# A two-layer graph network on one core: a new order of the normalisation's steps on VectorE and ScalarE

## The chip, the cores and the metric

The kernel runs on one core of one Trainium2 chip. The metric is the time of one execution in microseconds (us) on the device, lower is better. Five engines run side by side, each through its own list of instructions in order: TensorE (PE in the profile; PEld are its weight loads), VectorE (DVE), ScalarE (ACT), GpSimd (POOL) and SyncE (SP), which here issues nearly all DMAs. They are tied together by semaphores only: an instruction may wait until a semaphore has reached a count, and increments one when it ends.

## The reference

There are 1250 nodes of 512 features and 40000 edges. Cut to what matters:

```python
h = relu(layernorm(x))                                   # h0, layer 1's input
msg = (h[src] + edge_attr) @ Wm.T + bm
agg = segment_sum(msg, dst) / max(deg, 1)
o = h + gelu(concat(h, agg) @ Wu.T + bu)
x1 = x + layernorm(o) * gamma + beta
h1 = relu(layernorm(x1))                                 # layer 2's input
rst = (1 + eps) * h1 + segment_sum(h1[src], dst)
out = x1 + h1 + relu(rst @ W1 + b1) @ W2 + b2
```

All data is float32, and layernorm subtracts the mean and divides by sqrt(var + 1e-5) over the 512 features of a node.

## The kernel before

The nodes are cut into NT = 10 tiles of 128 rows (the last has 98). The kernel has four stages in time.

1. Up to about 243 us: a loop over 79 groups of 512 edges. TensorE sums the edge rows by destination and counts the edges between each pair of nodes into a 1280 x 1280 matrix of counts, A. The sums over neighbours of both layers are products with A (`piece`, `times_A`).
2. From 247 to 326 us: the normalisation, around which the change lies. Here all engines work tile by tile.
3. Up to 343 us: what is left of layer 2's products with A.
4. Up to the end: the two dense products of layer 2 (L1454, L1470), and the output.

In stage 2 TensorE's order is written out by hand (L1410 to L1437). For each tile b it runs `map_agg(b)` (L1401), the aggregate times the combined weights. From b = 5 on this is followed by `transpose_h1(b - 5)` (L1386) and, from b = 6, `times_A(b - 6, "A")` (L1377, L1378). Then, with the ten map_agg done, TensorE waits once for `t_ready` 10, that is for update(9), and for b = 5 to 9 runs `transpose_h1(b)`, `times_A(b - 1, "A")`, and one or two `times_A(.., "B")` as filler. `transpose_h1(b)` waits for h1(b); `times_A(b)` waits for low_h1(b), through the semaphore split1.

VectorE and ScalarE run software-pipelined rounds k. In each round they go through a fixed list of steps, each with a lag: a step with lag 2 works in round k on tile k - 2. For one tile the way is:

- VectorE `update` (L1017) forms t; ScalarE `gelu` (L627) and `h0_again` (L623, h0 once more from x, which SyncE loads again at L396).
- VectorE `add_h0` (L1022), `o_moments`, `o_moments2`, `o_variance` (L1026, L1030, L1034); GpSimd takes the power -1/2 (L463); VectorE `center` (L1038), and `add_x` (L1048), which gives x1 with the sum of its row; beside these, `add_beta` (L1042) makes x + beta ready.
- VectorE `x1_moments` (L1053) turns the row sum into minus the mean. ScalarE `x1_squares` (L632) sums the squares of x1 less its mean. VectorE `x1_variance` (L1057) waits for that sum; GpSimd takes the power (L460); VectorE `shift` (L1061) multiplies mean and power.
- ScalarE `h1` (L637) waits for shift and writes layer 2's input; `h1_high` (L641) rounds it to a high part. TensorE transposes it; ScalarE `h1T` (L646) copies the transpose; VectorE `low_h1` (L1066) makes the low part that times_A needs.

The lists of before, in their order, with the lags in brackets: ScalarE gelu (0), h0_again (0), x1_squares (2), h1 (3), h1_high (3), h1T (3); VectorE update (0), center (2), x1_variance (3), add_h0 (1), add_x (2), o_moments (1), x1_moments (2), shift (3), add_beta (1), o_moments2 (1), o_variance (1), low_h1 (4). So for one tile b ScalarE makes the squares in round b + 2 and h1 in round b + 3; VectorE makes x1_moments in its round b + 2, and variance and shift in its round b + 3. A step whose tile is out of range is left out: update and gelu end with round 9.

The waits of the steps that move:

```python
            def x1_variance(b):
                dve.wait_ge(x1_square, b + 1)
            def shift(b):
                dve.wait_ge(rs2_ready, b + 1)
            def x1_squares(b):
                act.wait_ge(x1_mean, b + 1)
            def h1(b):
                act.wait_ge(nb2_ready, b + 1)
                act.wait_ge(x1_square, b + 1)
```

Of the kernel before, what the change touches and what calls it, by code (L numbers as in the profile page):

```python
# [30 lines left out]
def gnn_kernel(nc, x, src, dst, edge, Wm, bm, Wu, bu, gamma, beta, W1, b1, W2, b2, eps, out):  # L31
# [20 lines left out]
    NX = NP // XW  # L52
    WU_ORDER = list(range(FC, 2 * FC)) + list(range(FC))
    assert ETAIL % 2 == 0 and ETAIL <= GE // 2 and D == GE and FC == 4 and sum(n for _, n in QS) == NP
    assert len(QS) == 3 and QS[2][1] * 2 == 512 and KW <= 256 and NT == 10

# [160 lines left out]
    with ctx:  # L217
# [198 lines left out]
        def _(pool):  # L416
# [16 lines left out]
            def add_sums_of(n):  # L433
                _, loaded = nc.values_load_multi_w_load_instructions(
                    offrow[0:1, n * 4:n * 4 + 2].bitcast(I32), engines=(mybir.EngineType.Pool,), min_val=0, max_val=(NP << 16) - 1,
                    skip_runtime_bounds_check_because="a pair of least indices of nodes")
                for half, first in enumerate((loaded[0] & 0xFFFF, loaded[0] >> 16)):
                    first = nc.s_assert_within(first, 0, NP - 1, skip_runtime_bounds_check_because="each is the least of indices of nodes")
                    cols = aggT[:, :, bass.ds(first, W)]
                    if half == 0:  # L440
                        pool.wait_ge(turned_out, n + 1)
                    if n > 0 or half > 0:
                        pool.wait_ge(early_step, n * 2 + half)
                    sums = turned_sums[n % TURNS][:].rearrange("p (f q) -> p f q", f=FC)[:, :, half * QUAD:half * QUAD + W]
                    nc.gpsimd.tensor_tensor(cols, sums, cols, ALU.add).then_inc(early_step, 1)  # L445
# [31 lines left out]
        def _(act):  # L477
# [138 lines left out]
            def full_conv(c):  # L616
                nc.scalar.copy(AR[:, c, :], A16[:, c, 0:NP]).then_inc(conv, 1)
# [35 lines left out]
            for c in range(1, CONV_AHEAD):  # L653
                full_conv(c)
            for k in range(NT + 4):
                for work, lag in ((gelu, 0), (h0_again, 0), (x1_squares, 2), (h1, 3), (h1_high, 3), (h1T, 3)):
                    if work is h0_again and k < 2:
                        continue
                    if 0 <= k - lag < NT:
                        work(k - lag)  # L660
                for c in range(CONV_AHEAD + 2 * k, min(CONV_AHEAD + 2 * k + 2, NT)):
                    full_conv(c)
# [15 lines left out]
        def _(dve):  # L678
# [68 lines left out]
            def offsets(n):  # L747
                _, loaded = nc.values_load_multi_w_load_instructions(
                    offrow[0:1, n * 4:n * 4 + 2].bitcast(I32), engines=(mybir.EngineType.DVE,), min_val=0, max_val=(NP << 16) - 1,
                    skip_runtime_bounds_check_because="a pair of least indices of nodes")  # L750
                return [nc.s_assert_within(first, 0, NP - 1, skip_runtime_bounds_check_because="each is the least of indices of nodes")
                        for first in (loaded[0] & 0xFFFF, loaded[0] >> 16)]
# [255 lines left out]
            def packed(first):  # L1008
                return ps[:, first:first + 2, :].rearrange("p k (g n) -> p (k g) n", g=2)

            def add_sums(products, start):
                part = aggT[:, :, start:start + products.shape[-1]]
                return V.tensor_tensor(part, products, part, ALU.add)
# [49 lines left out]
            def low_h1(b):  # L1063
# [4 lines left out]
            dve.wait_ge(late_in, 48)  # L1068
            dve.wait_ge(deg_step, 3 + NT)

            STEPS = [(update, 0), (center, 2), (x1_variance, 3), (add_h0, 1), (add_x, 2), (o_moments, 1), (x1_moments, 2), (shift, 3), (add_beta, 1),
                     (o_moments2, 1), (o_variance, 1), (low_h1, 4)]
            for k in range(NT + 5):
                if k == 5:
                    dve.wait_ge(piece_mm, 3 * NT)
                    add_sums(packed(0)[:, :, 0:LAST], QS[2][0]).then_inc(agg_done, 1)
                for work, lag in STEPS:
                    if 0 <= k - lag < NT:
# [28 lines left out]
        def _(pe):  # L1107
# [323 lines left out]
            for _, b in filler:  # L1431
                last = times_A(b, "B")
# [66 lines left out]
```

## Time and profile before

| | us |
|---|---|
| time, median of 3 runs | 483.59 (482.88 to 483.61) |
| the profiled execution's own time | 483.73 |
| its span in the trace | 481.9 |
| TensorE busy | 468.1 |
| VectorE busy | 260.6 |
| ScalarE busy | 172.0 |
| GpSimd busy | 123.3 |

The span runs from the first to the last instruction of the trace; some 1.8 us of the execution's time lie around it. Busy time is the sum over an engine's instructions, overlaps counted once. In a timeline each row gives the start of an instruction and its duration in us, the engine, the line of the kernel, the operation, what it writes and reads, and in square brackets how long its engine had been idle before it and what ended that. Instructions of one engine overlap a little: the next starts some 0.06 to 0.08 us before the end that is shown for the one before it. So the time that a step takes in its engine's row of work is read from start to start.

### The profile page before, as it was taken

To read this page: it belongs to the slowest core of one execution; us is meant where nothing else is said; L and a number is where in the kernel's file an instruction comes from. 1 tells how busy PE (TensorE), PEld (TensorE's weight loads), DVE (VectorE), ACT (ScalarE), POOL (GpSimd) and SP (SyncE) were. 2 spreads that over 40 slices of the span, in tenths; PEclk is the share of its full clock that TensorE was granted. 3 is DMA by queue.
4 is the path that set the end of the run, shared out by engine and by line. 5 is a ranking of instruction groups with operands and counts; after the bars stand their busy time and mean duration, and the time that the engine had idled before them with its cause. 6 is when DMAs were issued, how large, how long until landed. Compare 5 with 4: busy or idle time off the path is not lost.

```text
span 481.9 us, 9420 instructions
## 1 busy us (share of the span) xinstructions
PE 468.1 (97%) x3313; PEld 282.3 (59%) x3313; DVE 260.6 (54%) x615; ACT 172.0 (36%) x332; POOL 123.3 (26%) x185
## 2 busy tenths in 40 slices
PE   6999999999999999999999999899999999999997
PEld 5555555454555455788765755799744449444445
DVE  4799887778787877997847599822000000011011
ACT  6677642333333337521049387920021213000000
POOL 4016434443343422000000232449980000000000
PEclk9999999999999999999999999999999999999999
DMA  8999999999999999999430111030220000010111
GB/s 280 377 395 407 409 387 387 406 389 403 394 387 402 407 396 382 345 347 339 167 89 22 44 45 40 28 148 1 74 101 0 0 0 1 22 44 23 44 44 38
DMA packets 31832, 98.92 MB, mean 205 GB/s; under 512 B 3686, under 2 KB 4906, under 8 KB 31786
## 3 DMA queue, kind: packets, MB, share of 16 engines
q1 hardware_dynamic: 30570, 97.27, 53.4%
q10 hardware_dynamic: 1216, 1.05, 0.7%
q8 instruction: 27, 0.44, 0.4%
q14 instruction: 19, 0.16, 0.1%
HBM read 95.76 MB, written 2.56 MB: 204 GB/s over the span
## 4 chain that ended last, share of the span: by engine, by line
PE 89%; DVE 3%; issue 3%; DMA 2%; DVEq 1%; ACT 1%; SPq 0%; POOL 0%; ACTq 0%; POOLq 0%
PE ps L1470 14%; PE ps L1454 14%; PE ps L1185 11%; PE ps L1401 7%; PE ps L1234 7%; PE ps L1204 6%; PE ps L1377 4%; PE ps L1378 4%; PE ps L1295 4%; PE ps L1213 4%; PE ps L1296 4%; PE ps L1193 3%; PE ps L1137 3%; DMA WmN<-in_L_gnn_Wm_dram 2%; DVE A L760 1%
## 5 line engine op out<-in xcount | busy, mean ns | idle before, releaser
L445 POOL TENSOR_TENSOR aggT<-turned_sums,aggT 128x88 f32 x118 | 61.3, 520 | 96.7 <-ACT turned_sums L518 83.7
L760 DVE TENSOR_TENSOR A<-ps,A 128x220 f32 x158 | 60.8, 385 | 33.0 <-PE ps L1204 24.1
L1098 DVE TENSOR_TENSOR U<-ps,U 128x512 f32<-128x512 f32 x9 | 6.2, 692 | 122.3 <-PE ps L1470 122.3
L1470 PE MATMUL ps<-W2s,hid 128*128 128x512 f32 (+1 forms) x176 | 68.9, 553 | 0.0
L1454 PE MATMUL ps<-aggT,W1s 128*128 (+1 forms) x192 | 67.3, 513 | 0.0
L1185 PE MATMUL ps<-ea,oneD 128*22 128x256 f32 x944 | 62.6, 383 | 3.1 <-issue 2.8
L1454 PEld LDWEIGHTS ps<-aggT,W1s 128*128 128x128 f32 x192 | 36.4, 190 | 30.7 <-issue 30.6
L1470 PEld LDWEIGHTS ps<-W2s,hid 128*128 128x128 f32 (+1 forms) x176 | 32.6, 185 | 36.0 <-issue 34.5
L1185 PEld LDWEIGHTS ps<-ea,oneD 128*22 128x22 f32 x944 | 23.3, 101 | 50.0 <-issue 25.3
L512 ACT COPY packed_sums<-ps 128x256 f32<-128x256 f32 x59 | 22.0, 372 | 80.7 <-PE ps L1185 80.5
L1377 PE MATMUL ps<-AR,Hh 128*128 128x256 f32 (+2 forms) x160 | 43.8, 310 | 0.0
L1378 PE MATMUL ps<-AR,Hl 128*128 128x256 f32 (+2 forms) x160 | 43.0, 305 | 0.0
L739 DVE TENSOR_TENSOR oneK<-iotaP,P_key 128x1760 bf16<-128x1760 bf16 (+1 forms) x40 | 42.6, 1064 | 0.0
L669 ACT ACTIVATE hid<-ps,b1C 128x512 f32 (+1 forms) x24 | 14.6, 608 | 77.7 <-PE ps L1454 77.7
L1204 PE MATMUL ps<-oneK,oneS 128*128 128x220 bf16 x316 | 40.9, 260 | 0.4 <-DVE A L760 0.4
L1234 PE MATMUL ps<-Wu1T,U 128*128 128x512 f32 x80 | 41.3, 598 | 0.0
L1401 PE MATMUL ps<-CT,aggT 128*128 128x512 f32 x80 | 35.5, 592 | 0.0
L1295 PE MATMUL ps<-ARc,Hh 128*128 128x512 f32 x80 | 32.8, 410 | 0.7 <-DVE Hl L794 0.7
L1204 PEld LDWEIGHTS ps<-oneK,oneS 128*128 128x128 bf16 x316 | 29.9, 97 | 2.8 <-issue 1.0
L1296 PE MATMUL ps<-ARc,Hl 128*128 128x512 f32 x80 | 31.6, 394 | 0.0
L1378 PEld LDWEIGHTS ps<-AR,Hl 128*128 128x128 f32 x160 | 30.2, 189 | 1.7
L1377 PEld LDWEIGHTS ps<-AR,Hh 128*128 128x128 f32 x160 | 30.2, 189 | 1.6
(152 smaller groups left out, 631.5 us busy)
## 6 DMA issues: line engine op xcount, KB each, us to landing
ea<-in_edge_attr_dram SPq DMA_DIRECT2D x78, 1024.0 KB, 8.7
X<-in_x_dram SPq DMA_DIRECT2D x1, 2304.0 KB
xt<-in_x_dram SPq DMA_DIRECT2D x9, 256.0 KB, 2.5
out_dram<-U SPq DMA_DIRECT2D x9, 256.0 KB
W1s<-in_L_gnn_W_dram SPq DMA_DIRECT2D x1, 2048.0 KB, 9.0
W2s<-in_L_gnn_W_dram SPq DMA_DIRECT2D x1, 2048.0 KB, 8.4
Wu2N<-in_L_gnn_Wu_dram ACTq DMA_DIRECT2D x2, 512.0 KB, 4.2
WmN<-in_L_gnn_Wm_dram SPq DMA_DIRECT2D x1, 1024.0 KB, 7.3
```

The costliest lines, as they stand in the source:

```text
L445: nc.gpsimd.tensor_tensor(cols, sums, cols, ALU.add).then_inc(early_step, 1)
L760: V.tensor_tensor(cols, ps[:, 4 + m % 2, half * KW:(half + 1) * KW].rearrange("p (h w) -> p h w", w=W), cols, ALU.add).then_inc(add_step, 1)
L1185: last = T.matmul(to.rearrange("p (c d) -> p c d", c=2), oneD[h][:, g * 2 + j, :], data, start=j == 0, stop=j == 1)
L1204: last = T.matmul(ps[:, 4 + m % 2, (j // 2) * KW:(j // 2 + 1) * KW], sources[:, j // 2, :, j % 2], keys[:, j // 2, :, j % 2], start=j % 2 ...
L1234: quarter = T.matmul(ps[:, ASIDE_BANK["u1", b], :], U[:, b, f * P:(f + 1) * P], Wu1T[:, f, :], start=f == 0, stop=f == FC - 1)
L1295: T.matmul(to, Hh[:, c, rows], here, start=c == 0 and (q < 2 or f % 2 == 0), stop=False)
L1296: last = T.matmul(to, Hl[:, c, rows], here, start=False, stop=c == NT - 1 and (q < 2 or f % 2 == 1))
L1377: T.matmul(to, Hh[:, b, rows], AR[:, b, start:start + cols], start=b == 0 and (cols == 512 or f % 2 == 0), stop=False)
L1378: last = T.matmul(to, Hl[:, b, rows], AR[:, b, start:start + cols], start=False, stop=b == NT - 1 and (cols == 512 or f % 2 == 1))
L1401: last = T.matmul(ps[:, 2 + b % 2, :], aggT[:, f, b * P:(b + 1) * P], CT[:, f, :], start=f == 0, stop=f == FC - 1)
L1454: last = T.matmul(ps[:, CHUNK_BANK[k % 4], 0:cols], W1s[:, f, k * P:(k + 1) * P], aggT[:, f, bass.ds(start, cols)], start=f == 0, stop=f = ...
L1470: last = T.matmul(ps[0:rows, Y_BANK[b + half], 0:cols.stop - cols.start], hid[:, k, b * P:b * P + rows], W2s[:, k, cols], start=k == 0, st ...
```

## The change

Two lists are reordered, and nothing else changes: the same instructions, the same waits and the same data.

- ScalarE: x1_squares (of tile k - 2) moves behind h1 and h1_high (of tile k - 3).
- VectorE: x1_variance (k - 3) moves ahead of center; shift (k - 3) moves from behind x1_moments to ahead of add_x; x1_moments (k - 2) moves ahead of o_moments, to directly behind add_x.

```diff
-                for work, lag in ((gelu, 0), (h0_again, 0), (x1_squares, 2), (h1, 3), (h1_high, 3), (h1T, 3)):
+                for work, lag in ((gelu, 0), (h0_again, 0), (h1, 3), (h1_high, 3), (x1_squares, 2), (h1T, 3)):
...
-            STEPS = [(update, 0), (center, 2), (x1_variance, 3), (add_h0, 1), (add_x, 2), (o_moments, 1), (x1_moments, 2), (shift, 3), (add_beta, 1),
+            STEPS = [(update, 0), (x1_variance, 3), (center, 2), (add_h0, 1), (shift, 3), (add_x, 2), (x1_moments, 2), (o_moments, 1), (add_beta, 1),
                      (o_moments2, 1), (o_variance, 1), (low_h1, 4)]
```

## Rows read from the trace of the kernel before

**Rows 1.** The page's busy times: engine, busy us, share of the span, instructions.
```profile
PE 468.1 (97%) x3313; PEld 282.3 (59%) x3313; DVE 260.6 (54%) x615; ACT 172.0 (36%) x332; POOL 123.3 (26%) x185
```

**Rows 2.** Busy time of stages 2 and 3 together, with TensorE's granted clock (1.00 is full).
```profile
247.00:343.50 96.50, 94.28 (x523) 70.47 (x522) 57.96 (x139) 54.43 (x90) 38.83 (x38) 1.00 0.13 46
```

**Rows 3.** Timeline of TensorE: map_agg, transposes, first matmuls of times_A, tiles 1 to 8.
```profile
277.05 3.60 PE L1401 MATMUL ps<-CT,aggT 128*128 128x512 f32 x8
280.62 0.66 PE L1386 MATMUL ps<-ident,X 128*128 128x128 f32 x4
...
292.16 0.60 PE L1386 MATMUL ps<-ident,X 128*128 128x128 f32 x4
...
297.90 0.60 PE L1386 MATMUL ps<-ident,X 128*128 128x128 f32 x4
...
301.96 0.63 PE L1386 MATMUL ps<-ident,X 128*128 128x128 f32 x4 [1.59 <-issue]
...
306.00 0.66 PE L1386 MATMUL ps<-ident,X 128*128 128x128 f32 x4 [0.63 <-ACT X L637]
306.41 0.48 PE L1377 MATMUL ps<-AR,Hh 128*128 128x512 f32 x1
...
309.63 0.48 PE L1377 MATMUL ps<-AR,Hh 128*128 128x512 f32 x1
...
313.76 0.48 PE L1377 MATMUL ps<-AR,Hh 128*128 128x512 f32 x1
```

**Rows 4.** Timeline of ScalarE, round 7's h1T(4) and round 8.
```profile
298.54 0.69 ACT L646 ACTIVATE aggT<-ps,eps 128x512 f32<-128x512 f32 x1 [1.77 <-PE ps L1386]
...
300.35 0.71 ACT L632 ACTIVATE X<-U,mv 128x512 f32<-128x512 f32 x1
...
301.06 0.80 ACT L637 ACTIVATE X<-U,nb,rs 128x512 f32<-128x512 f32 x1
301.89 0.62 ACT L641 CAST Hh<-X 128x512 fp32r<-128x512 f32 x1
```

**Rows 5.** Timeline of VectorE, round 9: update(9) to low_h1(5).
```profile
299.23 0.74 DVE L1017 SCALAR_TENSOR_TENSOR tt<-ps,rdeg,U 128x512 f32<-128x512 f32 x1
299.89 0.74 DVE L1038 SCALAR_TENSOR_TENSOR tt<-tt,mv,gammaB 128x512 f32<-128x512 f32 x1
301.19 0.15 DVE L1057 TENSOR_SCALAR ve<-mv 128x1 f32<-128x1 f32 x1 [0.56 <-ACT X L632]
...
301.88 0.74 DVE L1048 SCALAR_TENSOR_TENSOR U<-tt,rs,xt 128x512 f32<-128x512 f32 x1
...
302.55 0.69 DVE L1026 BATCH_NORM_STATS2 stats<-tt 128x6 f32<-128x512 f32 x1
...
304.16 0.69 DVE L1066 TENSOR_TENSOR Hl<-X,Hh 128x512 fp32r<-128x512 f32 x1
```

**Rows 6.** Timeline of ScalarE, a cast with an operation right behind it.
```profile
218.03 0.62 ACT L562 CAST ARc<-A 128x512 fp32r<-128x512 uint16 x1 [1.25 <-PE ps L1296]
218.56 0.20 ACT L601 ACTIVATE eps<-epsC 128x1 f32<-128x1 f32 x1
```

**Rows 7.** Timeline of VectorE, low_h1(6) and round 11.
```profile
308.38 0.69 DVE L1066 TENSOR_TENSOR Hl<-X,Hh 128x512 fp32r<-128x512 f32 x1
308.99 0.74 DVE L1038 SCALAR_TENSOR_TENSOR tt<-tt,mv,gammaB 128x512 f32<-128x512 f32 x1
309.65 0.15 DVE L1057 TENSOR_SCALAR ve<-mv 128x1 f32<-128x1 f32 x1
309.77 0.75 DVE L1048 SCALAR_TENSOR_TENSOR U<-tt,rs,xt 128x512 f32<-128x512 f32 x1
...
310.57 0.15 DVE L1053 TENSOR_SCALAR mv<-x_sum 128x1 f32<-128x1 f32 x1
310.97 0.16 DVE L1061 TENSOR_TENSOR nb<-mv,rs 128x1 f32<-128x1 f32 x1 [0.25 <-POOL rs L460]
```

**Rows 8.** The page's DMA issues, second load of x: KB each, us to landing.
```profile
xt<-in_x_dram SPq DMA_DIRECT2D x9, 256.0 KB, 2.5
```

## The prediction, made before the changed kernel ran

> **What bounds the kernel now.** I read the page's busy times first, then the stage table, then the timelines of stage 2. TensorE is busy 97% of the span [rows 1]: only its idle time can be won, and a wait of another engine costs only what reaches TensorE. In stages 2 and 3 it is idle for 96.50 - 94.28 = 2.22 us, at the full granted clock of 1.00, its level of 2.4 GHz [rows 2]. The timeline shows where: 1.59 us before the transposes of tile 5, 0.63 us before those of tile 6, and before those of tile 1 a gap of 0.13 us that the matmuls' modelled ends hide (map_agg takes 3.44 us from start to start, 277.05 + 3.44 = 280.49, and they start at 280.62) [rows 3]. The first is marked "issue", but h1(5) ends at 301.06 + 0.80 = 301.86 and the transposes start 0.10 us later [rows 3, 4]: all three wait for ScalarE's h1. All three gone would give 2.35 us.
>
> So two chains matter. ScalarE is tied to TensorE: h1T(4) follows the transposes' start by 0.64 us, the three steps h1T, gelu and h0_again take 1.81 us, squares 0.71, h1 0.83 up to h1_high [rows 3, 4]. VectorE is nearly full too: in round 9 it idled 0.56 us, and that in x1_variance(6), which waited for squares(6): it starts 0.84 us after they do [rows 4, 5]. low_h1(6) starts at 308.38, is visible at about 308.38 + 0.69 + 0.10 = 309.17, and times_A(6) needs it at 309.63 [rows 3, 7]. Only 0.46 us of slack are there.
>
> **The change, part by part.** No instruction is added or removed. On ScalarE h1 comes 0.71 us earlier behind h0_again, the place of the squares. In return the squares come behind h1 and h1_high: 0.83 us plus the pitch from h1_high to the next operation. That pitch isn't in the trace, since h1T waits there; a cast of the same size was followed after 0.53 us [rows 6], and the upper bound is h1_high's whole 0.62 us. I take 0.53, so the squares are late by 1.36 us, less what the round as a whole gains.
>
> On VectorE x1_variance moves ahead of center, so it wants the squares 0.66 us earlier (299.23 to 299.89, one step of this size [rows 5]) and gets them later. Behind the blocked x1_variance stand center, add_h0, shift, add_x, the moments, add_beta, low_h1 and the next update. TensorE waits for two of these: update(9) and low_h1. The rest of the round: from x1_variance to low_h1 it took 304.16 - 301.19 = 2.97 us [rows 5]; center (0.66) now lies within; and x1_moments stands directly behind add_x, whose sum it needs: 310.57 - 309.77 = 0.80 us, where o_moments follows after 0.67 (301.88 to 302.55), so 0.13 more [rows 5, 7]. Together 3.76 us. shift needs GpSimd's power, 310.97 - 309.65 = 1.32 us after x1_variance [rows 7]; center, the 0.06 us of x1_variance and add_h0 (0.60, as low_h1's 0.61 [rows 7]) cover 1.32 to 1.33 of that, so I take no wait. If the power came 0.1 to 0.2 us later, each round would pay that; earlier wins nothing.
>
> On x1_moments the Trainium skill says otherwise (VectorE: DVE Perf Modes, section "The DRAIN you can't avoid"): a chain of operations with a semaphore after each took as long as one without. By that rule the move would cost 0.00 instead of 0.13 us in each of two rounds and the sum below would be 0.26 us less. The row of 0.80 us decides, since here the value comes from a second instruction that reads the accumulator.
>
> Now step by step, in the times of the trace. The transposes of tile 1 lose their wait of 0.13 us; TensorE is then unbroken up to tile 4's.
> - Tile 3's transposes at 292.16 - 0.13 = 292.03. The chain to VectorE is 0.64 + 1.81 + 0.83 + 0.53 + 0.84 = 4.65 us: x1_variance(5) at 296.68, low_h1(4) at 300.44, update(9) at 301.05, done at 301.79.
> - Tile 4's transposes at 297.77. h1(5) starts at 297.77 + 0.64 + 1.81 = 300.22 and ends at 301.02, so it no longer holds TensorE. Tile 5's transposes wait for t_ready 10 instead: 301.79 + 0.10 = 301.89, 0.07 us earlier than before. The wait has changed its owner.
> - x1_variance(6) at 297.77 + 4.65 = 302.42 (before 301.19). low_h1(5) at 306.18 (before 304.16).
> - h1(6): h1T(5) at 302.53, h1(6) at 304.34 to 305.14. TensorE comes free at 301.89 + 3.41 = 305.30 (the 3.41 from 301.96 to 306.00 less 0.63): transposes of tile 6 at 305.30, 0.70 us ahead of before. This is the change's gain.
> - times_A(5) could start 0.41 us later, at 305.71, but low_h1(5) is visible at 306.18 + 0.79 = 306.97: 1.26 us of new idle time, now 0.56 us behind before.
> - Round 10: squares(7) allow x1_variance(7) at 304.34 + 0.83 + 0.53 + 0.84 = 306.54, VectorE arrives at 306.18 + 0.61 = 306.79. low_h1(6) at 310.55, visible at 311.34. TensorE is at times_A(6) at 306.97 + 3.22 = 310.19 (3.22 from 306.41 to 309.63 [rows 3]): 1.15 us more idle time. times_A(6) at 311.34 against 309.63: 1.71 us late.
> - Round 11: x1_variance(8) at 311.16, shift(8) 1.32 us later, add_x(9) after 0.07, x1_moments(9) after 0.80, low_h1(7) at 313.40, visible at 314.19. TensorE wants it at 311.34 + 4.13 = 315.47 (309.63 to 313.76 [rows 3]). No wait there, nor at tile 8, where h1(8) starts at 312.66 behind shift(8): x1_variance(9) at 314.86, shift(9) at 316.18, low_h1(8) visible at 317.0 against 319.6.
>
> After that TensorE runs on without idle time, so 1.71 us stay. What else the late VectorE moves is covered. update(7) runs by about 290.3 (x1_variance(4), one tile of 5.74 us before 296.68, less 0.66), and map_agg(9) wants it at about 294.3. The load of x for tile 9, on SyncE behind add_x(6), is issued about 299.3 and lands 2.5 us later [rows 8], and h0_again(9) wants it at 303.6. W1's load, queued behind add_x(9), and GpSimd's additions behind low_h1(9) shift by 2 to 3 us and are wanted only after 343 us.
>
> Sum: profiled execution 483.73 + 1.71 = 485.44 us. The median of the runs is 0.14 us under that execution, so 485.3 us. Bounds of this sum: x1_moments at 0.67 instead of 0.80, -0.26; the pitch behind h1_high at 0.62, +0.09; power late by 0.2 us in two rounds, +0.4. That makes 485.0 to 485.8.
>
> A measurement of this kernel can tell about 0.2% (0.97 us) from no change: the bounds are 482.62 and 484.56 us.
>
> **The rivals.**
> 1. The change works as built: VectorE's delay never reaches TensorE, h1 is earlier and that counts. Place: low_h1(5) and (6). It decides where x1_variance stalls VectorE by under about 0.7 us in all. For it: rows 5 show only 0.56 us of stall now, and h1 is the one releaser that the profile names. Against it: the squares move by 1.36 us and the step that wants them by 0.66 the other way, and 0.46 us of slack is left. Time: the 0.70 us won at tile 6 stay, 483.59 - 0.70 = 482.9; all three gaps gone, 483.59 - 2.35 = 481.2. Chance 0.08, half of it below 482.62.
> 2. VectorE is late only once: it makes up the second stall, because the squares start sooner than my chain says, and times_A(6) finds its low part at 310.2. Then +0.56 to +0.8 stays: 484.2 to 484.4. Chance 0.08.
> 3. GpSimd's power becomes the bound of VectorE's rounds. The cover of 1.32 us equals the power's 1.32 us; with 0.3 us more in rounds 8 to 11 update(9), low_h1(5) and (6) shift in turn, +0.9 to +1.2 beyond my sum: 486.3. Chance 0.10.
> 4. The clock: two stalls of 1.26 and 1.15 us close to each other, and TensorE falls to its 1.2 GHz level. For it: no such pair is in the trace; against it: 1.59 and 0.63 us passed at 1.00. Price, an estimate: one tile of 4.13 us doubled, 485.3 + 4.1 = 489.4. The Trainium skill (TensorE: Matmul & The Clock Gate, Part 1) has such a fall after idleness. Chance 0.02.
>
> **How the numbers follow.** My forecast has 0.72, all of it slower. Rivals 3 and 4 are slower as well: 0.84. Rival 2 and half of rival 1 lie within 0.2%: 0.12. Faster: 0.04. The range takes in my bounds, the upper half of rival 2 and most of rival 3: 484.2 to 486.5.
>
> **What would show it.** x1_variance (L1057) waiting for ScalarE's squares earlier in the stage too, over 1 us for tile 2, and some 0.7 us in each of rounds 8 and 9; transposes of tile 5 released by update (L1017), those of tile 6 without an idle time of any size; times_A (L1377) with two new waits for low_h1 (L1066), each over 1 us; TensorE's idle time in stages 2 and 3 at about 3.9 us instead of 2.2. Wrong would be my forecast if L1377 shows no wait, or if L1061 waits for GpSimd in each round.

## The result, and the profile after

The changed kernel takes 485.51 us (median of 6 runs, 485.25 to 485.67) beside 483.65 us (6 runs) for the kernel before on the same chip: ratio 1.0038, 95% interval 1.0028 to 1.0049. It is slower, by 1.86 us. I had forecast 485.3 us. The profiled execution took 485.67 us, its span 483.9 us.

The page's busy times of the changed kernel, and then the row of its stage table for stages 2 and 3 (busy time of each engine in a stretch of the trace), answering to [rows 1, 2]:

```profile
PE 469.0 (97%) x3313; PEld 282.7 (58%) x3313; DVE 261.1 (54%) x615; ACT 171.9 (36%) x332; POOL 124.0 (26%) x185
```

```profile
247.00:345.60 98.60, 95.12 (x524) 71.00 (x523) 58.99 (x140) 54.28 (x90) 39.23 (x38) 1.00 0.14 45
```

Every engine has as many instructions as before. TensorE's idle time in stages 2 and 3 rose from 2.22 to 98.60 - 95.12 = 3.48 us, and the granted clock stayed at 1.00. Those 1.26 us are less than the loss: the ends of matmuls are modelled, so part of each wait counts as busy time (95.12 us against 94.28). Below I therefore measure from start to start. TensorE's timeline (answering to [rows 3]):

```profile
276.90 0.60 PE L1386 MATMUL ps<-ident,X 128*128 128x128 f32 x4
...
280.78 0.60 PE L1386 MATMUL ps<-ident,X 128*128 128x128 f32 x4
...
298.00 0.60 PE L1386 MATMUL ps<-ident,X 128*128 128x128 f32 x4
...
302.06 0.66 PE L1386 MATMUL ps<-ident,X 128*128 128x128 f32 x4 [1.59 <-DVE tt L1017]
...
305.43 0.66 PE L1386 MATMUL ps<-ident,X 128*128 128x128 f32 x4
...
307.13 0.50 PE L1377 MATMUL ps<-AR,Hh 128*128 128x512 f32 x1 [1.05 <-DVE Hl L1066]
...
311.48 0.50 PE L1377 MATMUL ps<-AR,Hh 128*128 128x512 f32 x1 [0.83 <-DVE Hl L1066]
...
315.69 0.48 PE L1377 MATMUL ps<-AR,Hh 128*128 128x512 f32 x1
...
319.47 0.60 PE L1386 MATMUL ps<-ident,X 128*128 128x128 f32 x4
```

Tile 5's transposes still wait for 1.59 us, but now for update(9) (L1017). Tile 6's have lost their gap. Two waits for low_h1 (L1066) are new, at times_A(5) and (6). VectorE's rounds 9 to 11 show why (answering to [rows 5, 7]):

```profile
301.26 0.74 DVE L1017 SCALAR_TENSOR_TENSOR tt<-ps,rdeg,U 128x512 f32<-128x512 f32 x1
302.65 0.15 DVE L1057 TENSOR_SCALAR ve<-mv 128x1 f32<-128x1 f32 x1 [0.64 <-ACT X L632]
302.72 0.74 DVE L1038 SCALAR_TENSOR_TENSOR tt<-tt,mv,gammaB 128x512 f32<-128x512 f32 x1
...
304.05 0.74 DVE L1048 SCALAR_TENSOR_TENSOR U<-tt,rs,xt 128x512 f32<-128x512 f32 x1
...
304.84 0.16 DVE L1053 TENSOR_SCALAR mv<-x_sum 128x1 f32<-128x1 f32 x1
304.91 0.68 DVE L1026 BATCH_NORM_STATS2 stats<-tt 128x6 f32<-128x512 f32 x1
...
306.39 0.69 DVE L1066 TENSOR_TENSOR Hl<-X,Hh 128x512 fp32r<-128x512 f32 x1
307.00 0.15 DVE L1057 TENSOR_SCALAR ve<-mv 128x1 f32<-128x1 f32 x1
...
310.73 0.69 DVE L1066 TENSOR_TENSOR Hl<-X,Hh 128x512 fp32r<-128x512 f32 x1
...
312.58 0.16 DVE L1061 TENSOR_TENSOR nb<-mv,rs 128x1 f32<-128x1 f32 x1 [0.44 <-POOL rs L460]
...
313.57 0.69 DVE L1066 TENSOR_TENSOR Hl<-X,Hh 128x512 fp32r<-128x512 f32 x1
```

x1_variance(6) stood still 0.64 us for the squares, with center and all else behind it. low_h1(5) came 3.74 us after it, against 2.97 before. ScalarE's round 8 (answering to [rows 4]):

```profile
298.63 0.69 ACT L646 ACTIVATE aggT<-ps,eps 128x512 f32<-128x512 f32 x1 [1.75 <-PE ps L1386]
...
300.45 0.80 ACT L637 ACTIVATE X<-U,nb,rs 128x512 f32<-128x512 f32 x1
301.28 0.62 ACT L641 CAST Hh<-X 128x512 fp32r<-128x512 f32 x1
301.81 0.72 ACT L632 ACTIVATE X<-U,mv 128x512 f32<-128x512 f32 x1
```

h1(5) starts 1.82 us behind h1T(4), where the squares stood, and the squares 1.36 us behind h1(5).

**A measure for what follows.** Tile 0's transposes start at 276.61 us before and at 276.90 after: 0.29 us that the change doesn't make: they are there already at the first add_h0 (L1022, 257.06 against 257.35), ahead of the first step that it moves. Over all profiles of this case they start between 276.28 and 277.04. So I compare the stretch from tile 0's to tile 9's transposes, the "stretch" below. Before it is 317.53 - 276.61 = 40.92 us, after 319.47 - 276.90 = 42.57 us: +1.65. With the 0.29 that is 1.94 us, the difference of the two profiled executions (485.67 - 483.73). The kernel before was profiled once, so how far its own stretch repeats is not shown; the changed kernel's does to 0.01 us.

### The profile page after: what moved, and what is told of

It reads as the page before. It is cut to its first block, busy times and chain, and to the rows that moved or that the text cites. A ratio compares the mean times of both kernels' runs of the same rounds, so it can differ in the third digit from the quotient of the medians.

```text
span 483.9 us, 9420 instructions
## 1 busy us (share of the span) xinstructions
PE 469.0 (97%) x3313; PEld 282.7 (58%) x3313; DVE 261.1 (54%) x615; ACT 171.9 (36%) x332; POOL 124.0 (26%) x185
## 3 DMA queue, kind: packets, MB, share of 16 engines
q10 hardware_dynamic: 1216, 1.05, 0.7%
## 4 chain that ended last, share of the span: by engine, by line
PE 89%; DVE 5%; issue 3%; DMA 2%; ACT 1%; DVEq 1%; SPq 0%; POOL 0%; ACTq 0%; POOLq 0%
PE ps L1470 14%; PE ps L1454 14%; PE ps L1185 11%; PE ps L1401 7%; PE ps L1234 6%; PE ps L1204 6%; PE ps L1295 4%; PE ps L1213 4%; PE ps L1377 4%; PE ps L1296 4%; PE ps L1378 4%; PE ps L1193 3%; PE ps L1137 3%; DMA WmN<-in_L_gnn_Wm_dram 2%; DVE A L760 1%
## 5 line engine op out<-in xcount | busy, mean ns | idle before, releaser
L463 POOL TENSOR_TENSOR rs<-ve,mhalf 128x1 f32<-128x1 f32 x10 | 7.9, 787 | 96.8 <-DVE ve L1034 96.8
```

## The experiments

All are timed against the kernel before on the same chip. In all edited runs but two only the lists of steps of ScalarE and VectorE differ, so an edit is given by the list that differs.

| kernel | ratio (95% interval) | stretch, us | against before |
|---|---|---|---|
| changed, first profile | 1.0038 (1.0028 to 1.0049) | 42.57 | +1.65 |
| changed, again | 1.0033 (1.0022 to 1.0044) | 42.56 | +1.64 |
| ScalarE's order alone | 1.0018 (1.0009 to 1.0027) | 41.87 | +0.95 |
| VectorE's order alone | 1.0009 (1.0000 to 1.0018) | 41.38 | +0.46 |
| changed, squares before h1_high | 1.0015 (1.0006 to 1.0024) | 41.86 | +0.94 |
| changed, squares last | 1.0279 (1.0249 to 1.0308) | 55.73 | +14.81 |
| changed, x1_moments back | 1.0032 (1.0020 to 1.0043) | 42.33 | +1.41 |
| changed, low_h1 early | 1.0030 (1.0019 to 1.0042) | 42.37 | +1.45 |
| changed, wait for update(9) moved | 1.0038 (1.0023 to 1.0052) | 42.95 | +2.03 |
| new order, both engines | 0.9970 (0.9958 to 0.9982) | 39.64 | -1.28 |
| new order, wait moved too | 0.9968 (0.9956 to 0.9980) | 39.70 | -1.22 |
| new order on ScalarE alone | 1.0021 (1.0011 to 1.0031) | 41.75 | +0.83 |
| new order on VectorE alone | 1.0000 (0.9991 to 1.0009) | 41.04 | +0.12 |

### Each half of the change by itself

ScalarE's new list with VectorE's old one:

```diff
-(gelu, 0), (h0_again, 0), (x1_squares, 2), (h1, 3), (h1_high, 3), (h1T, 3)
+(gelu, 0), (h0_again, 0), (h1, 3), (h1_high, 3), (x1_squares, 2), (h1T, 3)
```

> ScalarE's new order alone (squares behind h1 and h1_high); VectorE keeps the order of before. Theory A (the later squares hold up x1_variance, and low_h1 behind it reaches TensorE late): h1(5) is ready 0.8 to 0.9 us earlier, but x1_variance(6) waits for the squares until about 302.4 and from there VectorE needs 2.97 us to low_h1(5): TensorE gets a wait of about 0.3 us at times_A(5), one of about 0.3 us at times_A(6), and h1(7) is late by about 0.9 us because its squares are; in sum 0.8 us slower than before, the ratio about 1.0016. Rival B (only VectorE's new order costs; ScalarE's is the gain of 0.7 us): 0.7 us faster, no wait of TensorE for low_h1.

And VectorE's new list with ScalarE's old one:

```diff
-(update, 0), (center, 2), (x1_variance, 3), (add_h0, 1), (add_x, 2), (o_moments, 1), (x1_moments, 2), (shift, 3), (add_beta, 1), ...
+(update, 0), (x1_variance, 3), (center, 2), (add_h0, 1), (shift, 3), (add_x, 2), (x1_moments, 2), (o_moments, 1), (add_beta, 1), ...
```

> VectorE's new order alone; ScalarE keeps the order of before. Theory A: the squares come as early as before, so x1_variance(6) runs at about 301.2; but center now lies behind it and x1_moments waits for add_x, so low_h1 comes 0.66 + 0.11 us later in each round: TensorE keeps its waits for h1(5) and h1(6) (about 1.6 and 0.7 us), and gets small ones at h1(7) and low_h1(6), together 0.4 to 0.5 us; 0.5 us slower than before, ratio 1.0010. Rival B (VectorE's new order is the cause of the whole loss): 1.9 us slower, ratio 1.0038. The two parts of the change should add up to less than the 1.9 us of the whole, about 1.3.

Measured: +0.95 and +0.46 us in the stretch. In the whole time the first is slower (1.0009 to 1.0027), the second only just (1.0000 to 1.0018). Rival B falls, since ScalarE's half wins nothing. ScalarE alone, TensorE's waits and then, from VectorE's timeline, x1_variance in round 9:

```profile
301.17 0.63 PE L1386 MATMUL ps<-ident,X 128*128 128x128 f32 x4 [0.88 <-DVE tt L1017]
...
305.54 0.66 PE L1386 MATMUL ps<-ident,X 128*128 128x128 f32 x4 [0.97 <-ACT X L637]
...
309.96 0.66 PE L1386 MATMUL ps<-ident,X 128*128 128x128 f32 x4 [0.69 <-ACT X L637]
```

```profile
302.47 0.15 DVE L1057 TENSOR_SCALAR ve<-mv 128x1 f32<-128x1 f32 x1 [0.76 <-ACT X L632]
```

Tile 5's transposes come 0.9 us sooner into the stretch (24.45 us after tile 0's against 25.35), as was intended. But the late squares of one tile make the variance and so the next h1 late, and the gap returns at tiles 6 and 7. The waits of about 0.3 us for low_h1 that I expected at times_A(5) and (6) show in the weight loads only (0.24 and 0.23 us); the larger waits are for h1. VectorE alone keeps before's gaps of 1.59 and 0.63 us and has a small loss behind them. The halves add up to 1.41 us; 0.24 us arise only together.

### How late the squares are

The changed kernel with one step moved on ScalarE, first sooner, then later:

```diff
-(gelu, 0), (h0_again, 0), (h1, 3), (h1_high, 3), (x1_squares, 2), (h1T, 3)
+(gelu, 0), (h0_again, 0), (h1, 3), (x1_squares, 2), (h1_high, 3), (h1T, 3)
```

> The changed kernel with one step moved: ScalarE's squares directly behind h1, ahead of h1_high, so that they start 0.53 us sooner. Theory A (what counts is when the squares end): x1_variance(5) and (6) run 0.5 us earlier, update(9) too, so TensorE's wait before tile 5's transposes falls from 1.59 to about 1.1 us; the loss against before falls by 0.5 to 0.6 us to about 1.3 us (ratio 1.0027). Rival C (the loss is VectorE's own longer round, center ahead of low_h1 and x1_moments in the wake of add_x, and not the squares): no difference to the changed kernel, ratio 1.0038.

```diff
-(gelu, 0), (h0_again, 0), (h1, 3), (h1_high, 3), (x1_squares, 2), (h1T, 3)
+(gelu, 0), (h0_again, 0), (h1, 3), (h1_high, 3), (h1T, 3), (x1_squares, 2)
```

> The disputed cost made larger: the changed kernel with ScalarE's squares behind h1T too. h1T waits for TensorE's transposes, so the squares are late by a further 1.5 to 2 us in each round up to tile 4. Theory A: x1_variance blocks VectorE for longer in each round, low_h1 is late from tile 0 on, TensorE waits at every times_A and for more than 4 us at update(9): 8 to 10 us slower than before, ratio 1.018 to 1.020. Rival C: no more than the changed kernel, ratio 1.004.

Sooner: the loss in the stretch falls by 0.71 us, somewhat more than the 0.5 to 0.6 forecast. The squares start 0.70 us behind h1, where h1_high started 0.83 us behind it, since they don't wait for h1's end. Rival C falls as the cause of the whole. Later: +14.81 us, far beyond my 8 to 10. The mechanism is the expected one: x1_variance waited 23.2 us for the squares in all against 4.2 in the changed kernel, and TensorE 4.75 us for update(9). It waited at only four of the times_A, though, and the longest of these waits, 2.46 us at times_A(0), was for VectorE's addition for layer 1 (L1013), which stood behind the blocked list too. What I had left out is the clock. The stage table of that kernel, one row after each of these two waits (the clock is the third number from the end):

```profile
286.00:288.00 2.00, 2.00 (x5) 1.15 (x4) 1.97 (x7) 1.53 (x3) 0.00 (x0) 0.50 0.16 22
...
310.30:316.00 5.70, 5.68 (x19) 4.91 (x20) 3.07 (x9) 4.05 (x7) 0.99 (x1) 0.50 0.00 0
```

Three steps of TensorE ran without any wait but longer than before: from times_A(0) to tile 2's transposes 291.16 - 284.12 = 7.04 us against 286.42 - 281.04 = 5.38, from tile 5's to tile 6's transposes 5.93 against 3.41, from times_A(6) to tile 8's transposes 328.16 - 322.80 = 5.36 against 3.77. That is 5.8 us of clock. Simply taken off, they leave 9.0 us for the waits, within the 8 to 10; no run separates the two.

### x1_moments and low_h1

The changed kernel with x1_moments behind o_moments again:

```diff
-(shift, 3), (add_x, 2), (x1_moments, 2), (o_moments, 1), (add_beta, 1)
+(shift, 3), (add_x, 2), (o_moments, 1), (x1_moments, 2), (add_beta, 1)
```

> The changed kernel with x1_moments back behind o_moments, so that it no longer waits in the wake of add_x; squares and x1_variance as changed. From the rows of the changed kernel add_x, x1_moments, o_moments take 0.85 us from start to start against 0.73 in the old order. Theory A: x1_variance to low_h1 falls from 3.75 to 3.64 us, and twice that (rounds 9 and 10) reaches TensorE: from tile 0's to tile 9's transposes 0.2 us less than in the changed kernel, 1.4 to 1.45 us more than before. Rival C (such waits behind a chained step, of which there is one in each of ten rounds, are what the change costs): at least 1 us less. In the whole time 0.2 us is under what a measurement tells; the stretch of the trace decides.

Measured: the loss is 0.24 us smaller in the stretch (the two profiles of the changed kernel agree within 0.01), and from x1_variance(6) to low_h1(5) it takes 3.62 us instead of 3.74:

```profile
302.78 0.15 DVE L1057 TENSOR_SCALAR ve<-mv 128x1 f32<-128x1 f32 x1 [0.77 <-ACT X L632]
...
306.40 0.69 DVE L1066 TENSOR_TENSOR Hl<-X,Hh 128x512 fp32r<-128x512 f32 x1
```

0.12 us in each of two rounds bear out the term of 0.13. The Trainium skill (VectorE: DVE Perf Modes, section "The DRAIN you can't avoid") found that a semaphore after each of eight copies costs nothing extra. This trace doesn't agree for x1_moments behind add_x. That the sum comes from an accumulator is not shown to be the reason: in the kernel before, add_x starts 309.77 - 308.99 = 0.78 us after the center that it waits for, with only x1_variance between them, where center's 0.66 and x1_variance's 0.06 us make 0.72 [rows 7].

The changed kernel with low_h1 directly behind x1_moments:

```diff
-(x1_moments, 2), (o_moments, 1), (add_beta, 1), (o_moments2, 1), (o_variance, 1), (low_h1, 4)
+(x1_moments, 2), (low_h1, 4), (o_moments, 1), (add_beta, 1), (o_moments2, 1), (o_variance, 1)
```

> The changed kernel with low_h1 directly behind x1_moments, 2.1 us earlier in VectorE's round. Theory A with its queue read narrowly (low_h1 is late because four small and two large steps stand between): the two waits at times_A go and with them 1.7 us of the loss, ratio about 1.000. Theory A with the loop between the engines (squares, variance, power, shift, h1 and again squares): the waits at times_A fall to 0.2 us, but TensorE then waits for h1(7) by about 1.4 us and for h1(8) by 0.6 us, and the loss stays at 1.5 us, ratio 1.003.

Measured: of the waits for low_h1 two of about 0.2 us are left, seen in the weight loads only, and TensorE waits for h1 instead; the loss is +1.45 us. Its timeline:

```profile
302.07 0.66 PE L1386 MATMUL ps<-ident,X 128*128 128x128 f32 x4 [1.60 <-DVE tt L1017]
...
309.91 0.66 PE L1386 MATMUL ps<-ident,X 128*128 128x128 f32 x4 [1.05 <-ACT X L637]
...
314.75 0.66 PE L1386 MATMUL ps<-ident,X 128*128 128x128 f32 x4 [0.15 <-ACT X L637]
```

So low_h1 is not what is late by itself. Late is the loop squares, variance, power, shift, h1, squares, and in the changed kernel low_h1 is where TensorE meets it first. But the edit adds to the loop too. o_variance now stands directly ahead of x1_variance in VectorE's list, and GpSimd takes their two powers in that order. VectorE's shift(7) and shift(8), and GpSimd's powers ahead of shift(7), in this run:

```profile
308.85 0.16 DVE L1061 TENSOR_TENSOR nb<-mv,rs 128x1 f32<-128x1 f32 x1 [0.44 <-POOL rs L460]
...
313.68 0.16 DVE L1061 TENSOR_TENSOR nb<-mv,rs 128x1 f32<-128x1 f32 x1 [0.96 <-POOL rs L460]
```

```profile
307.17 1.05 POOL L463 TENSOR_TENSOR rs<-ve,mhalf 128x1 f32<-128x1 f32 x1 [3.29 <-DVE ve L1034]
308.19 0.63 POOL L460 TENSOR_TENSOR rs<-ve,mhalf 128x1 f32<-128x1 f32 x1
```

In the changed kernel shift(7) didn't wait and shift(8) waited 0.44 us. So the 1.45 us are those of this order, with up to 0.44 us of GpSimd's queue in the wait for h1(7), and not the bare price of the loop.

### The wait for update(9)

On TensorE, with the changed kernel's lists:

```diff
-            pe.wait_ge(t_ready, NT)
             filler = [("B", b) for b in range(NT)]
             for b in range(5, NT):
                 transpose_h1(b)
                 times_A(b - 1, "A")
+                if b == 5:
+                    pe.wait_ge(t_ready, NT)
```

> The changed kernel, with TensorE's wait for update(9) moved from ahead of tile 5's transposes to ahead of the first filler product, which is the first to write the banks that update reads. The wait of 1.59 us before tile 5's transposes then ends with h1(5), 0.7 us sooner. Theory A: what sets the end is low_h1(6) on VectorE's own chain from the squares of tile 6; these follow h1T(5), gelu and h1(6) no sooner, so times_A(5) and (6) wait longer by what was won, and the time stays at the changed kernel's, within 0.1 us; ratio 1.0035 to 1.004. Rival E (the wait for update(9) is where the change's gain was lost): 0.7 us less than the changed kernel, ratio 1.002.

TensorE's timeline in this run:

```profile
300.82 0.66 PE L1386 MATMUL ps<-ident,X 128*128 128x128 f32 x4 [0.84 <-ACT X L637]
...
304.70 0.66 PE L1386 MATMUL ps<-ident,X 128*128 128x128 f32 x4 [0.43 <-ACT X L637]
...
306.66 0.50 PE L1377 MATMUL ps<-AR,Hh 128*128 128x512 f32 x1 [1.31 <-DVE Hl L1066]
...
311.12 0.60 PE L1386 MATMUL ps<-ident,X 128*128 128x128 f32 x4
```

The ratio is the changed kernel's, 1.0038. Tile 5's transposes came 0.76 us sooner (24.40 us after tile 0's against 25.16), and low_h1(6) not at all (33.84 us after them against 33.83). In this profile the clock interfered too: it was granted at 0.50 from about 307.5 to 310.8 us, and times_A(5) with its filler took 311.12 - 306.66 = 4.46 us instead of 310.05 - 307.13 = 2.92. So the stretch of +2.03 isn't clean; the start of low_h1(6) and the ratio are the verdict against rival E. The clock doesn't decide that ratio: three of the five executions show a mean clock of 1.0, and they took 485.29, 485.43 and 485.58 us.

### An order that beats both

If the loop is what binds, h1 and squares have to come early together, and on VectorE the members of the loop ahead of what only feeds the next tile:

```diff
-(gelu, 0), (h0_again, 0), (x1_squares, 2), (h1, 3), (h1_high, 3), (h1T, 3)
+(h1, 3), (x1_squares, 2), (gelu, 0), (h0_again, 0), (h1_high, 3), (h1T, 3)
...
-(update, 0), (center, 2), (x1_variance, 3), (add_h0, 1), (add_x, 2), (o_moments, 1), (x1_moments, 2), (shift, 3), (add_beta, 1), (o_moments2, 1), (o_variance, 1), (low_h1, 4)
+(center, 2), (x1_variance, 3), (update, 0), (add_x, 2), (add_h0, 1), (x1_moments, 2), (shift, 3), (o_moments, 1), (low_h1, 4), (o_moments2, 1), (o_variance, 1), (add_beta, 1)
```

> A new order by theory A. ScalarE: h1, x1_squares, gelu, h0_again, h1_high, h1T, so that both h1 and the squares come ahead of gelu and h0_again. VectorE: center, x1_variance, update, add_x, add_h0, x1_moments, shift, o_moments, low_h1, o_moments2, o_variance, add_beta, so that nothing that TensorE doesn't wait for stands ahead of low_h1. Theory A: no wait for low_h1 and nearly none for h1; only update(9) holds tile 5's transposes by about 1.4 us; 1.1 to 1.4 us faster than before, ratio 0.9975. Rival D (h1 ahead of gelu and h0_again delays gelu, add_h0 and so the whole next tile): slower than before, with VectorE waiting for gelu at L1022.

Measured: 482.53 us beside 483.83, ratio 0.9970 (0.9958 to 0.9982), 1.3 us faster than before. Rival D falls, since VectorE's only wait at add_h0 (L1022) is the one of 2.2 us for gelu at tile 0, as before. TensorE's timeline at tiles 5, 6 and 7, and then VectorE's round 9, where x1_variance(6) comes without a wait:

```profile
301.12 0.66 PE L1386 MATMUL ps<-ident,X 128*128 128x128 f32 x4 [1.25 <-DVE tt L1017]
...
304.40 0.60 PE L1386 MATMUL ps<-ident,X 128*128 128x128 f32 x4
...
307.63 0.66 PE L1386 MATMUL ps<-ident,X 128*128 128x128 f32 x4
```

```profile
300.26 0.15 DVE L1057 TENSOR_SCALAR ve<-mv 128x1 f32<-128x1 f32 x1
300.32 0.74 DVE L1017 SCALAR_TENSOR_TENSOR tt<-ps,rdeg,U 128x512 f32<-128x512 f32 x1
...
302.99 0.68 DVE L1066 TENSOR_TENSOR Hl<-X,Hh 128x512 fp32r<-128x512 f32 x1
```

The same with TensorE's wait for update(9) moved:

> The new order of the run that was faster than before (both h1 and squares ahead of gelu; low_h1 early), with TensorE's wait for update(9) moved behind times_A(4) as well. Theory A: its 1.25 us before tile 5's transposes go, but VectorE, idle for 0.6 us only between tiles 4 and 8, sets when shift(6) and shift(7) come, so TensorE waits for h1(6) by 0.4 us and for h1(7) by 1.0 us instead; no gain on the kernel with the wait in place: 1.3 us faster than before, ratio 0.997. Rival E (the wait is worth its length): 2.5 us faster than before, ratio 0.9948.

Measured: nothing more is won (-1.22 us in the stretch). Tile 5's wait of 1.25 us is gone, and its transposes start at 299.94 as soon as TensorE is free; tiles 6 and 7 wait for h1 instead:

```profile
299.94 0.60 PE L1386 MATMUL ps<-ident,X 128*128 128x128 f32 x4
...
303.61 0.66 PE L1386 MATMUL ps<-ident,X 128*128 128x128 f32 x4 [0.26 <-ACT X L637]
...
307.87 0.66 PE L1386 MATMUL ps<-ident,X 128*128 128x128 f32 x4 [0.82 <-ACT X L637]
```

The new lists one at a time, and the changed kernel once more:

> Only ScalarE's half of the new order: h1, x1_squares, gelu, h0_again, h1_high, h1T; VectorE as before. Theory A: h1 ahead of gelu comes as soon as shift is there, but shift stands where it stood, behind add_x, and now sets h1(6) and h1(7); TensorE waits about 1.2 and 1.5 us for these, about 0.3 us twice for low_h1; 0.8 us slower than before, ratio 1.0017. Rival F (ScalarE's half is what won): 1.3 us faster.

> Only VectorE's half of the new order: center, x1_variance, update, add_x, add_h0, x1_moments, shift, o_moments, low_h1, and the rest; ScalarE as before. Theory A: h1 stays behind the squares and behind h1T's chain, so TensorE's waits for h1(5) and h1(6) stay at 1.6 and 0.7 us; within 0.1 us of before, ratio 1.000. Rival F' (VectorE's half is what won): 1.3 us faster.

> The changed kernel once more, beside the others on the same chip, as the measure of how far two executions' stretches agree: from tile 0's to tile 9's transposes 42.57 us as in its first profile, ratio 1.0035 to 1.004.

Measured: +0.83 and +0.12 us, so that neither half wins anything and the two together win 1.28 us. With ScalarE's half alone h1(6) and h1(7) wait for shift (TensorE's gaps there are 0.99 and 1.28 us). I had put this down to shift's old place in the list; the trace shows a second reason, which is rival D's. h0_again now comes behind h1 and the squares, and VectorE's add_h0, which stands ahead of shift, waits for it at five tiles, at this one for example:

```profile
301.77 0.69 DVE L1022 TENSOR_TENSOR tt<-tt,h0t 128x512 f32<-128x512 f32 x1 [0.77 <-ACT h0t L623]
```

shift(6) follows at 303.71, so it is late by these 0.77 us too. In the new order on both engines add_h0 stands behind update and add_x, and doesn't wait. With VectorE's half alone h1 gains nothing, since it stands in ScalarE's list behind the squares: h1(6) starts 304.93 - 302.92 = 2.01 us after shift(6), against 305.14 - 303.20 = 1.94 before. Tile 5's transposes wait for update(9) instead, for 1.68 us. The changed kernel repeats its stretch to 0.01 us, with its three waits at 1.59, 1.06 and 0.86 us.

## Why the prediction was right

The forecast of 1.71 us was made for the stage; the stretch gave 1.65. The steps, with 0.29 us taken off the times after:

| step | predicted | measured |
|---|---|---|
| tile 5's transposes, released by update(9) | 301.89 | 301.77 |
| x1_variance(6) | 302.42 | 302.36 |
| tile 6's transposes | 305.30 | 305.14 |
| low_h1(5) | 306.18 | 306.10 |
| times_A(5) | 306.97 | 306.84 |
| low_h1(6) | 310.55 | 310.44 |
| times_A(6) | 311.34 | 311.19 |
| low_h1(7) | 313.40 | 313.28 |

- The unseen pitch from h1_high to the squares: 0.53 taken, 0.53 measured (301.28 to 301.81).
- x1_moments in the wake of add_x: 0.80 taken, 0.79 measured, and the 3.76 us from x1_variance to low_h1 were 3.74. Putting it back confirmed its share, though not the reason given for it (the accumulator).
- The power covered by center and add_h0 in rounds 9 and 10: right, shift (L1061) first waits in round 11, for 0.44 us, where add_h0 is out of range. Rival 3 isn't seen. I took the power's 1.32 us for shift(9) as well, where it was only 315.81 - 315.00 = 0.81 us; TensorE had time to spare there.
- TensorE's new waits: 1.26 and 1.15 us. The view shows 1.05 and 0.83 idle because a matmul's modelled end lies behind the point at which the next could have started; from start to start, with the paces of before (0.41 us from the transposes to times_A, 3.22 us from times_A(5) to times_A(6)), they are 307.13 - (305.43 + 0.41) = 1.29 and 311.48 - (307.13 + 3.22) = 1.13 us. For the same reason idle time was 3.48 us and not the 3.9 I expected.
- Off by little, and evened out: TensorE reached times_A(6) 0.15 us sooner than forecast, in part because low_h1 was visible after 0.74 us instead of 0.79. From there to tile 8's transposes it took 315.33 - 311.48 = 3.85 us instead of before's 3.77. That the stretch comes within 0.06 us is in part luck.
- Off: I took x1_variance to be held by the squares at tile 4 too. It wasn't: after the wait of 1.58 us at tile 2 VectorE was so far behind that tiles 3 and 4 found the squares ready, and at tile 5 0.27 us were left instead of 0.7. This changed nothing behind it, since update(9) hangs on the squares of tile 5 either way.
- Off in the telling: I told the loss as a list in front of low_h1. The run with low_h1 early lost nearly as much through shift and h1 (1.45 against 1.65 us), part of it by GpSimd's order.
- The 0.2 us by which the whole time exceeds my 485.3 are of the size by which the time up to the stretch differs between executions (0.29 in these two profiles).

Rival 1, the change working as built, was wrong at the point named for it: VectorE's delay at low_h1(5) was 306.10 - 304.16 = 1.94 us against the 0.7 named there. Rival 2, one late round only, fell with the second wait of 1.13 us. Rival 4's fall of the clock did not happen in the changed kernel, but it lies near: it happened with the wait moved.

## What to carry to other kernels

When two engines work in rounds and hand a small value back and forth, write down the loop (here squares, variance, power, shift, h1) and count its length in every engine's list, the small engine's too; moving a consumer ahead in one list while its producer moves back in the other lengthens it from both ends. Here the reorder had to be made on both engines at once: each half of the better order alone gave nothing or lost 0.8 us, both together won 1.3. And the wait that the profile shows last is where the loop touches the critical engine, not what to cut: taking away the wait for update(9), or for low_h1, brought up another of nearly the same total.

## What the hardware showed that I had not expected

TensorE's granted clock fell from its 2.4 GHz level to the 1.2 GHz level (0.50) after waits that are short beside the whole. With the wait for update(9) moved, it had been idle for 0.84, 0.43 and 1.31 us between 300 and 307 us; then this kernel's stage table shows (TensorE's busy time is the second number, the clock the third from the end):

```profile
305.00:307.00 2.00, 0.69 (x6) 0.41 (x5) 1.97 (x7) 1.58 (x4) 0.93 (x2) 1.00 0.00 0
307.00:308.00 1.00, 1.00 (x5) 0.80 (x4) 1.00 (x4) 0.00 (x0) 0.74 (x2) 0.71 0.00 0
308.00:309.00 1.00, 1.00 (x4) 0.81 (x3) 0.96 (x4) 0.93 (x2) 0.00 (x0) 0.50 0.00 0
...
311.00:312.00 1.00, 1.00 (x9) 0.93 (x8) 0.67 (x2) 0.25 (x1) 1.00 (x2) 1.00 0.00 0
```

It cost 1.54 us over one step, of which the following wait took back 1.1. The changed kernel had idle times of 1.59, 1.05 and 0.83 us, no less in sum, and stayed at 1.00 in both of its profiles. Nor does the order alone decide it: of the five executions with the wait moved, the profiled one shows a mean clock of 0.996, the others 0.999 and three times 1.0. What tells them apart was not tried.
